# Sums moved from VectorE to TensorE, output and comparison operands moved to ScalarE, and all queues in a new order

## The reference

```
h = relu(tanh(conv9(x) * scale) + bias)            # 367 rows of 128 per batch
h = h + attention(layernorm(h))                    # three windows, radius 12, 84, 90
h = h + ffn(layernorm(h))
attention: scores = q k' / sqrt(128); acc = mean over windows of softmax(masked scores) @ x
           out = layernorm(x + acc @ Wo + bo) * gamma + beta
ffn:       q = layernorm(h Wq' + bq) in 8 heads of 64, two halves of 32 each
           s0, s1 = cosine of each half with 64 keys; top 16 of each
           top 16 of the sums of pairs; expert index = sum of the two key indices
           out = sum over heads and picks of gelu(h . down[index]) * softmax weight * up[index]
```

## Time and profile before

| what | us |
|---|---|
| median of 3 runs | 1349.89 (1349.42 to 1351.28) |
| profiled execution | 1352.16 |
| its span, first to last instruction | 1350.4 |
| VectorE busy | 1243.1 (92%) |
| TensorE busy (products) | 995.4 (74%) |
| GpSimd busy | 905.9 (67%) |
| ScalarE busy | 771.1 (57%) |

### The profile page before, as it was taken

The page is one execution under the profiler, slowest core; times in us unless marked ns, Lnnn a source line. Parts: engine busy times, 40 slices in busy tenths (PEclk is TensorE's granted clock), DMA queues, the critical chain, the costliest instruction groups (busy, mean ns, idle before and its releaser), DMA issues.

```text
span 1350.4 us, 38006 instructions
## 1 busy us (share of the span) xinstructions
PE 995.4 (74%) x10065; PEld 760.4 (56%) x10065; DVE 1243.1 (92%) x9664; ACT 771.1 (57%) x2115; POOL 905.9 (67%) x1926
## 2 busy tenths in 40 slices
PE   3855858778777786877878686877878777787644
PEld 2634646557556564765656475656747555564533
DVE  4339696999999999999999999999999999999995
ACT  2555747475574756657575665756566475745322
POOL 4338574767767677686767768676776867667551
PEclk7868877767788787767878787777768788776655
DMA  2020000000000000000000000000000000000000
GB/s 51 7 34 9 9 13 9 14 10 6 13 13 13 10 16 10 7 13 13 14 10 9 17 6 13 10 17 9 7 20 6 14 4 17 4 6 15 6 7 7
DMA packets 36073, 16.53 MB, mean 12 GB/s; under 512 B 15792, under 2 KB 35648, under 8 KB 35858
## 3 DMA queue, kind: packets, MB, share of 16 engines
q1 hardware_dynamic: 35234, 13.82, 4.2%
q10 hardware_dynamic: 624, 0.30, 0.1%
HBM read 7.59 MB, written 6.01 MB: 10 GB/s over the span
## 4 chain that ended last, share of the span: by engine, by line
DVE 63%; issue 11%; POOL 9%; PE 7%; ACT 6%; SPq 2%; DMA 0%; DVEq 0%; POOLq 0%; ACTq 0%
DVE idx L1593 17%; DVE val L1591 12%; DVE scores L1596 9%; DVE cr L1664 7%; DVE oh L1606 5%; DVE best L1662 4%; DVE wl L1626 2%; POOL qscale L679 2%; DVE masked L1546 2%; DVE bns L1516 2%; PE banks L1222 1%; PE bankM L1344 1%; ACT act_g L939 1%; DVE prod L1635 1%; ACT probs L887 1%
## 5 line engine op out<-in xcount | busy, mean ns | idle before, releaser
L1593 DVE FIND_INDEX8 idx<-val,scores 128x8 uint16<-128x64 f32 x1472 | 292.1, 217 | 0.0
L1591 DVE MAX8 val<-scores 128x8 f32<-128x64 f32 x1472 | 201.7, 208 | 0.0
L1344 PE MATMUL bankM<-wl,oh 128*128 128x16 f16 x5888 | 160.6, 172 | 29.3 <-DVE wl L1626 23.9
L1344 PEld LDWEIGHTS bankM<-wl,oh 128*128 128x128 f16 x5888 | 161.5, 101 | 32.0 <-DVE wl L1626 25.9
L679 POOL TENSOR_TENSOR qscale<-nmx,power 128x16 f32<-128x16 f32 x46 | 137.5, 2990 | 52.7 <-DVE nmx L1570 52.7
L1596 DVE MATCH_REPLACE8 scores<-val,scores 128x64 f32<-128x64 f32 x736 | 145.4, 208 | 0.0
L1606 DVE TENSOR_SCALAR oh<-eh 128x1024 f16<-128x1024 int16 x368 | 133.0, 429 | 3.1 <-ACT eh L1023 3.1
L1307 PE MATMUL bankS<-wgk,hnT 128*128 128x512 f32 x184 | 127.2, 781 | 0.0
L1352 PE MATMUL bankM<-up_x,prod 128*128 128x128 f32 x368 | 80.9, 390 | 46.4 <-DVE prod L1635 46.3
L1023 ACT ACTIVATE eh<-bankM,digit_bias 128x256 int16<-128x256 f32 x184 | 72.7, 489 | 69.1 <-PE bankM L1329 69.1
L1222 PEld LDWEIGHTS banks<-diag,probs 124*124 124x124 f32 x672 | 106.1, 243 | 9.4 <-issue 6.8
(11 more groups left out here) (204 smaller groups left out, 2866.6 us busy)
## 6 DMA issues: line engine op xcount, KB each, us to landing
h_in<-h_rows SPq DMA_DIRECT2D x45, 64.0 KB, 2.6
out<-o_sb SPq DMA_DIRECT2D x45, 64.0 KB, 1.5
x_in<-in_x SPq DMA_DIRECT2D x16, 93.8 KB
x_in<-in_x SPq DMA_DIRECT2D x16, 62.5 KB
h_rows<-hsum SPq DMA_DIRECT2D x16, 62.0 KB
h_rows<-hsum SPq DMA_DIRECT2D x16, 61.0 KB
h_rows<-hsum SPq DMA_DIRECT2D x16, 60.5 KB
x_in<-in_x SPq DMA_DIRECT2D x16, 31.0 KB
```

Of the source, the lines that this page charges most:

```text
L1344: last = e.matmul(coef[:, g, :, :], oh[:, k, g, :, :].rearrange("p v t -> p (v t)"), wl[:, part, k, :, TG * g:TG * (g + 1)], start=k + par ...
L1591: last = v.max(out=v_[:, hd, s, best8], in_=src[:, hd, s, :])
L1593: last = v.max_index(out=i_[:, hd, s, best8], in_max=v_[:, hd, s, best8], in_values=src[:, hd, s, :])
```

## The change

- `res` becomes part of PSUM bank C. `p1_wo` adds xb there by a second product, identity times xb, and waits for xb. `p1_res` and its semaphore are gone; the statistics and the layer norm read PSUM.
- `experts_out` adds `h_in` in PSUM by a product with the identity times 4096, and waits for `h_in`. `finish` is a copy with a scale on ScalarE.
- There are eight shifted copies `eh` instead of four. `one_high` does two values in each half instead of four, each over twice as many elements.
- `el` and `lows` are gone. ScalarE makes `low_same`, for each l of 0 to 3 the number 4 * high + l, from the first copy in `eh`, and `one_low` compares `expert` with it.
- All five `body` functions have a new order. The steps of the preparation are moved in it as well.

```diff
-SHIFTS = 4
+SHIFTS = 8
...
-        res = sb("res", [NT, 3, D])
...
+        res = bankC[0:NT, D:4 * D].rearrange("p (t d) -> p t d", d=D)
...
 SP body
+                each(fetch, c + -1, 0)
+                each(store, c + -2, 0)
                 each(store, c + -2, 1)
-                each(fetch, c + -1, 0)
                 each(store, c + -2, 2)
                 do(keep, c)
                 each(fetch, c + -1, 1)
                 each(fetch, c + -1, 2)
-                each(store, c + -1, 0)
...
 ScalarE
+            def finish(c, t):
+                b, m = c.b, c.flat(t)
+                act.wait_ge(ffn_done, m + 1)
+                wait(act, stored[c.third(t)], 16 * c.turn(t))
+                a.activation(o_sb[:, c.third(t), :], ffn, ACT.Copy, scale=1.0 / WSCALE).then_inc(out_ready, 1)
...
                 for j in range(SHIFTS):
                     last = a.activation(eh[:, j, :, :], merged[:, :, 2 * QT:3 * QT], ACT.Identity, bias=digit_bias[:, j:j + 1], scale=1.0 / EL)
                 last.then_inc(high_ready, 1)
+                act.wait_ge(high_ready, 2 * n + 1)
+                for l in range(EL):
+                    a.activation(low_same[:, :, l, :], eh[:, 0, :, :], ACT.Identity, bias=low_bias[:, l:l + 1], scale=float(EL))
                 a.activation(expert[:, :, :], merged[:, :, 2 * QT:3 * QT], ACT.Copy).then_inc(high_ready, 1)
...
 TensorE
             def p1_wo(c, t):
                 b, n = c.b, c.tile(t)
                 pe.wait_ge(axT_ready, n + 1)
-                e.matmul(bankC[0:NT, (1 + t) * D:(2 + t) * D], axT[:, :], wo_sb[:, :], start=True, stop=True).then_inc(wo_done, 1)
+                if t == 0:
+                    pe.wait_ge(xb_ready, c.b + 1)
+                out_t = bankC[0:NT, (1 + t) * D:(2 + t) * D]
+                e.matmul(out_t, axT[:, :], wo_sb[:, :], start=True, stop=False)
+                e.matmul(out_t, id32[0:NT, 0:NT], xb[:, t, :], start=False, stop=True).then_inc(wo_done, 1)
...
                 pe.wait_ge(prod_ready, m + 1)
+                pe.wait_ge(h_back[c.third(t)], 16 * (c.turn(t) + 1))
                 for l in range(EL):
-                    last = e.matmul(ffn, prod[:, l, :], up_x[:, l, :], start=l == 0, stop=l == EL - 1)
+                    last = e.matmul(ffn, prod[:, l, :], up_x[:, l, :], start=l == 0, stop=False)
+                last = e.matmul(ffn, id_scaled[0:QT, 0:QT], h_in[:, c.third(t), :], start=False, stop=True)
                 last.then_inc(ffn_done, 1)
...
 VectorE
-            def p1_res(c):
-                b = c.b
-                dve.wait_ge(wo_done, 3 * (b + 1))
-                dve.wait_ge(xb_ready, b + 1)
-                wait(dve, xh_ready, b)
-                v.tensor_tensor(res[:, :, :].rearrange("p t d -> p (t d)"), bankC[0:NT, D:4 * D],
-                                xb[:, :, :].rearrange("p t d -> p (t d)"), ALU.add).then_inc(res_ready, 1)
...
-                v.tensor_scalar(el[:, :, :], expert[:, :, :], EL - 1, None, ALU.bitwise_and).then_inc(digits_ready, 1)
-                dve.wait_ge(digits_ready, m + 1)
...
-                v.tensor_tensor(ol[:, :, :, :], el[:, :, :].unsqueeze(2).to_broadcast([128, 2, EL, QT]),
-                                lows[:, :, :].unsqueeze(1).to_broadcast([128, 2, EL, QT]), ALU.is_equal).then_inc(wl_ready, 1)
+                v.tensor_tensor(ol[:, :, :, :], expert[:, :, :].unsqueeze(2).to_broadcast([128, 2, EL, QT]), low_same[:, :, :, :], ALU.is_equal)\
+                 .then_inc(wl_ready, 1)
...
-            def finish(c, t):
-                b, m = c.b, c.flat(t)
-                dve.wait_ge(ffn_done, m + 1)
...
```

224 lines of the change are left out of this document (108 added, 116 removed).

## The result

The changed kernel takes 1343.19 us (median of five, 1339.22 to 1344.29), the kernel before in the same comparison 1351.28 us. The ratio is 0.9939, interval 0.9922 to 0.9957: faster by 8 us. The forecast was 1319 us, 32 less than before, in a range of 1301 to 1342. So the sign is right, the size a quarter of what was forecast, and the time lies 1 us above the range.

The account below looks back on a forecast made before the run. VectorE was taken to bound the kernel, busy 1243.1 of 1350.4 us. Savings -46.0, start +2, filling +4, middle waits +6 and end +3 sum to -31 us: 1319 from a median of 1349.9, range 1301 to 1342.

Parts of the forecast that it names:

- The start, +2: First 100 us: convolution behind turn_weights delays the chain 5.8 us, mostly given back; net 2 us more, bounds -1 and +8.
- The 3.4 for the scores of batch 1: Start: batch 1's scores, now looked at after half a ranking, leave VectorE waiting for exponentials, 2 to 5 us, taken as 3.4.
- Filling, +4: 100 to 300 us, batches 0 and 1: longer chain and partly waited-out savings cost 4 us, bounds 0 and 9.
- VectorE's savings, 46 us: Work leaving VectorE: res 8.8, o_sb 12.7, el 10.0, wider comparison oh 14.5; together 46.0 us.
- Waits in the middle, 0.5 us a batch: New waits, chiefly q_guard late by up to 2 us; 0.5 a batch taken, 6 us, bounds nothing and 26.
- GpSimd "gets nothing": GpSimd gets no added work from the change and rises to 75% busy in the middle; costed at nothing.
- rival (d): Second tile's std chain makes q_guard late every batch; 2.4 us a batch erases the gain, 3.6 gives 1366 us; chance 0.10.
- the marker of 0.71: Sign in the profile after: comparison oh in 184 instructions of about 0.71 us; 0.85 us would refute the forecast.
- rival (b): The wider comparison oh on VectorE gains nothing: 1333 us; chance 0.08.
- Rival (c): ScalarE's queue becomes narrow: 3.2 us before wm half seen in one tile of three, 1.5 us a batch, 1339 us; chance 0.14.
- The end, +3: Last tile's comparison waits longer for eight copies, low_same and weights: 3 us more, bounds 1 and 5.

Follow-up runs that it names:

- the good start: Changed kernel with the convolution of batch 0 ahead of turn_weights and its wsq ahead of key_norms, as before the change: 1333.93 us.
- the two reduced kernels: Changed kernel with the earlier convolution and el back on VectorE: with four copies 1354.28 us, with eight 1348.02 us.
- the kernels with the wait: GpSimd's select of a first tile waits for one_high of the tile before: four copies, el back 1344.71 us; eight, el back 1338.94; p1_norm moved 1331.05.

## Why the prediction was wrong

The runs form a chain, one group of edits at a step: before 1351; attention sum and output in the old orders 1337.4 (-14); the same in the new orders, with the good start, 1354.3 (+17); comparison and low digit there 1333.9 (-20); the new order of the start 1343.2 (+9). The forecast had -21.5, nothing, -24.5, +2 and 13 for waits.

The forecast was -46 us of work on VectorE and +15 of waits. The difference of the two profiled executions, after less before, can be split in the same way (us, rounded), since every microsecond of the span is one in which VectorE works or stands still:

| stretch | works | stands still | forecast for standing still |
|---|---|---|---|
| to the scores of batch 4 | -10.1 | +14.2 | +6 (start and filling) |
| batches 4 to 15 | -27.2 | +9.9 | +6 |
| the rest | -3.4 | +3.3 | +3 |
| sum | -40.8 | +27.4 | +15 |

So the steps that failed are the waits, 12.4 us too small, 8.2 of these in the start and filling, and the savings, 5 us too large. These make some 17.5 of the 24 us by which the forecast was off; some 5 more are the distance between the profiled execution and the median, which stays open. The forecast also counted 1 us twice: the 0.55 of res given back at the start and the 0.5 of the comparison and el at the end stand in the 46 as well.

- **The start, +2.** This is the largest miss. The delay of 5 to 6 us by the convolution was foreseen and came (5.2). What gives back was overestimated: the first MAX8 begins at 89.79, not 88.9, and what was late by 5.2 at the first masked scores is late by 7.6 at the second and 5.8 at the fourth batch. Undoing the order of the convolution gave 9.3 us by the medians and 6.4 in the profiled spans, so the forecast was off by 4 to 7 here. The 3.4 for the scores of batch 1 was no cost: the run that undoes it gains nothing.
- **Filling, +4.** Two steps wait 1.92 + 1.65 = 3.6 us each for ScalarE at oh and rden, 0.3 before. That makes 6 to 7, and VectorE is idle between 100 and 300 us for 12.5 us more in all, part of it time that the edits saved there.
- **VectorE's savings, 46 us.** Right in kind, too large. Durations were counted where slots count: after o_sb (276 ns) the next instruction starts 0.20 us later, after res (548) 0.465. By slots the two edits are worth 46 x 0.20 + 16 x 0.465 = 16.6 us instead of 21.5, and 14 were measured. The comparison goes from slots of 335 ns to 604 ns, 368 x 0.335 - 184 x 0.604 = 12 instead of 14.5. With 10 for el that makes 38.6. The overlap of neighbours was seen in oh, and it was not applied to the other groups.
- **Waits in the middle, 0.5 us a batch.** 0.83 more than before (in six batches VectorE is idle for 7.1 us instead of 2.2), and 2.7 of these 4.9 us are the wait of the statistics for h, a cause that the prediction had not named. With 2.5 us of slots less instead of 3, a batch gains 1.57, not 2.5: 10 us over the 11 batches. Batches are 77.8 us apart, not 76.4 to 77.
- **GpSimd "gets nothing".** This was put at nothing without a reason. By instruction counts it holds; by its time it does not. GpSimd's busy time went up by 48 us, 39 of them between 400 and 1200 us in the four groups shown above, and the run with four copies shows that this comes with the new orders, not with the width of the comparison. In the changed kernel VectorE's comparisons keep their lengths (oh 686 ns, ol 682), and what reaches VectorE is the wait for h, 5.1 us between 400 and 1200; the run that takes it away gains 2 us, inside the intervals. So in this kernel the step cost little of what was missing. In the two reduced kernels, where VectorE's comparisons are the ones that grow, one wait was worth 9 to 10 us. The prediction followed the moves of the orders for data that come late (the std of the second tile, rival (d)) and never asked which instructions of the two engines now run side by side. nmx does not wait in the middle, so (d) falls.
- **The wide comparison and ScalarE's copies.** The mean of 686 ns is just under the marker of 0.71, so rival (b) falls as far as VectorE's own time goes; how much of its 12 us the time shows is open (2 to 8 us, by the run with four copies). Rival (c), 3.2 us before wm half seen in every batch, did not come in the middle: oh does not wait there. It came in the old orders (24, 18 and 84 us) and, in the changed kernel, while filling.
- **The end, +3.** The last comparison waits 7.30 us instead of 2.26, and the waits of o_sb (5.4) are gone from VectorE; in all it stands still 3.3 us longer from the scores of batch 15 on. As forecast. From the first search of the last tile to the end it takes 48.3 us, 49.1 before.

The time came out near that of (c), 1339, by other causes than (c)'s.

## What to carry to other kernels

When an order is laid out anew, look not only at what comes late but at which instructions of VectorE and GpSimd come to run side by side, and which of them grow. It matters when they are VectorE's. A saving on a full engine is the time from its start to the next start, not its duration, and it is only as large as the queue that feeds it allows: test every edit alone in the old order and the new order with few edits, since here two edits alone in the old order (1337.4) beat all four as they were laid out (1343.2), and the same two in the new order lost everything (1354.3). An instruction put behind a wait for weights at the start should be one that needs them.

## What the runs showed of the hardware

Instructions of GpSimd and VectorE that run together can hold each other up, and not in proportion to their size. A GpSimd multiplication of 124x3 lasted 1.83 us instead of 0.2 and ended with the comparison beside it; ol of 128x1024 lasted 1.31 us instead of 0.69 behind a GpSimd product that had begun before it; a VectorE instruction of 124x3, lnm, took 441 ns on the mean in the old orders and 168 in the new ones (it lasted 0.83 us where GpSimd's wcell had begun 0.13 us before it); and with one wait that moved the products, 451 and 901 ns became 420 and 692, while wl beside them went from 683 to 809. To be side by side is not enough: in the kernel before, qscale runs beside eight comparisons and lasts 2.9 to 3.0 us, and they keep their 0.42.

The Trainium skill has this in "SBUF — State Buffer", section "SBUF: two separate sides": GpSimd and VectorE share a pair of ports, VectorE needs it in the modes that use two ports or with two inputs in SBUF (the latter only against a GpSimd instruction that reads SBUF), whoever starts first has it for the whole instruction, and the other stands. The rows of ol, wcell and wnorm agree with it. wnorm ends where the comparison ends. ol ends 0.54 us after wcell, and wcell 0.81 us after el, both a little less than their own lengths (0.69 and 0.95). Those of qscale don't: it began 2.6 us ahead of oh and lasts 4.24 us instead of 2.9, until oh and el have ended, so something of it is held up at its end. Nor does the order of the starts tell who goes first. In the kernels with the wait, wcell begins 0.25 us behind the first of two wl; in one (1344.71 us) it ends first and the second wl lasts 1.43 us, in the other (1331.05 us) both wl keep their 0.68 and wcell lasts 1.84. Why is open.

Which operations take the pair is only partly shown here: comparisons of 16 bits and products with two inputs do, and the many MAX8 and MATCH_REPLACE8 beside the same GpSimd instructions kept their lengths (207 to 208 ns on the mean from 400 to 1200 us, in the kernel before and in that of 1354.28 us).
